# Softmax denominators of a two-layer kernel: partial sums by adding DMAs, one product with ones per pair of heads

## The reference, cut to what matters

```
xn = layernorm(x)                                  # (8, 512, 128)
q = (xn @ Wq + bq).reshape(8, 512, 16, 64); k = xn @ Wk + bk; v = xn @ Wv + bv
w = softmax(einsum('bshd,btd->bhst', q, k) / 8, axis=-1)
out = einsum('bhst,btd->bshd', w, v).reshape(8, 512, 1024) @ Wo + bo
```

## Time and profile before

| | |
|---|---|
| Runs | median 1379.54 us of 3 (1374.84 to 1380.76) |
| Profiled execution | 1377.28 us, its span 1375.2 us, mean granted TensorE clock 0.962 |
| TensorE, matmuls | 91% busy, 7185 instructions |
| VectorE | 74% busy, 2393 instructions |
| ScalarE, GpSimd | 49% and 19% busy |
| DMA | 133.80 MB, mean 97 GB/s |
| Chain that ended last | TensorE 66%, VectorE 21%, issue 5%, ScalarE 3%, DMA 2% |

### The profile page before, as it was taken

One profiled execution on the slowest core, in us unless ns is written; L12 is line 12 of the kernel. 1 busy time (PEld: TensorE's weight loads), 2 busy tenths in 40 slices (PEclk: granted clock), 3 DMA queues, 4 the chain that ended last, 5 costly groups with the idle time before them and its releaser, 6 DMA issues.

```text
span 1375.2 us, 21811 instructions
## 1 busy us (share of the span) xinstructions
PE 1248.2 (91%) x7185; PEld 728.6 (53%) x7185; DVE 1016.0 (74%) x2393; ACT 673.7 (49%) x1252; POOL 262.9 (19%) x314
## 2 busy tenths in 40 slices
PE   4559899998999999999999999999999989999997
PEld 2335445554555455545554555455545558686844
DVE  7777878578857785788587767777677758686875
ACT  3126545534554345434643464345534458676741
POOL 3023222200120012001200120012000206363640
PEclk9559999999999999999999999999999999999999
DMA  2063655222312131224211321132212356465462
GB/s 77 0 169 93 186 170 179 54 58 56 110 46 66 41 116 42 54 49 112 63 49 48 118 64 49 48 90 76 62 44 53 95 162 230 156 227 173 144 203 63
DMA packets 89779, 133.80 MB, mean 97 GB/s; under 512 B 33293, under 2 KB 49229, under 8 KB 85701
## 3 DMA queue, kind: packets, MB, share of 16 engines
q1 hardware_dynamic: 75108, 99.80, 25.5%
q0 software_dynamic: 11344, 31.64, 7.0%
q10 hardware_dynamic: 3216, 0.97, 0.3%
HBM read 59.86 MB, written 38.68 MB: 72 GB/s over the span
## 4 chain that ended last, share of the span: by engine, by line
PE 66%; DVE 21%; issue 5%; ACT 3%; DMA 2%; SPq 2%; POOL 1%; ACTq 0%; DVEq 0%; POOLq 0%
PE bank L1458 14%; PE bank L1430 6%; PE bank L1469 6%; PE bank L1384 5%; PE bank L1431 5%; PE bank L1290 4%; DVE mneg L1022 4%; PE bank L1490 4%; PE bank L1292 4%; PE bank L1291 4%; DVE q_lm L1014 3%; PE bank L1306 2%; PE bank L1296 2%; PE bank L1341 2%; PE bank L1331 1%
## 5 line engine op out<-in xcount | busy, mean ns | idle before, releaser
L844 ACT ACTIVATE wide<-bank 128x512 f32<-128x512 f32 x512 | 296.4, 602 | 470.5 <-PE bank L1431 440.7
L1022 DVE TENSOR_REDUCE mneg<-bank 128x1 f32<-128x512 f32 x512 | 330.0, 685 | 154.5 <-PE bank L1384 147.8
L1458 PE MATMUL bank<-wide,v_w 128*32 128x512 f32 x2048 | 254.1, 615 | 0.8 <-issue 0.8
L1430 PE MATMUL bank<-q_hh,k_hl 128*128 128x512 f32 x512 | 235.7, 460 | 11.0 <-ACT wide L844 9.5
L1431 PE MATMUL bank<-q_lm,k_h 65*128 65x512 f32 x512 | 204.6, 400 | 0.0
L1430 PEld LDWEIGHTS bank<-q_hh,k_hl 128*128 128x128 f32 x512 | 97.1, 190 | 138.3 <-issue 84.0
L636 POOL TENSOR_TENSOR rs<-rs,power 128x4 f32<-128x4 f32 x24 | 24.5, 1021 | 663.3 <-DVE rs L918 663.2
L1469 PE MATMUL bank<-wide,ones 128*32 128x512 f32 x992 | 130.0, 596 | 0.0
L707 POOL DMA_INDIRECT y_rows<-y_m,to_u x92 | 99.1, 1077 | 128.6 <-DVE y_m L1148 106.6
L1458 PEld LDWEIGHTS bank<-wide,v_w 128*32 128x32 f32 x2048 | 54.5, 111 | 126.6 <-issue 121.4
L1384 PE MATMUL bank<-k_b,q_x 128*128 128x512 f32 x256 | 104.1, 407 | 9.6 <-issue 5.1
(11 more groups left out here) (238 smaller groups left out, 1953.3 us busy)
## 6 DMA issues: line engine op xcount, KB each, us to landing
q_hh<-q_x SPq DMA_DIRECT2D x256, 128.0 KB
w_t<-w_rows SPq DMA_DIRECT2D x23, 1024.0 KB
x_rows<-part_h POOLq DMA_DIRECT2D x65, 258.0 KB, 5.0
inv<-inverse_scratch SPq DMA_DIRECT2D x124, 128.0 KB, 3.0
w_rows<-w_t SPq DMA_DIRECT2D x8, 1024.0 KB, 5.1
x_m<-x_rows SPq DMA_DIRECT2D x23, 258.0 KB
stage<-in_L_ffn_W SPq DMA_DIRECT2D x16, 256.0 KB, 4.7
yab<-y_rows POOLq DMA_DIRECT2D x8, 512.0 KB, 7.7
```

What stands on the lines that cost most here:

```text
L844: act.activation(wide[:, st.g % WIDE, :], ps, ACT.Exp, scale=SCALE1).then_inc(wide_full, 1)
L1022: dve.tensor_reduce(mneg[:, pair % 2, col:col + 1], ps[:], X, ALU.max, negate=True).then_inc(free, 1)
L1430: pe.matmul(ps, k_hl[:, n, t], q_hh[:, gh % HEADS, :], start=True, stop=False)
L1458: pe.matmul(ps_out[0][rows, :], v_w[:, n, c, TILE * d:TILE * d + TILE], weights, start=(c == 0), stop=(c == TT - 1))
```

## The change

In the first 54 pairs (`added`) the four quarters' exponentials are added up before they meet the ones. The first quarter of both heads is written into `total`, two buffers of 128x2x512 that lie where `part_h` lies (the expert tiles' buffer, not in use yet). GpSimd adds the other three quarters to it with DMAs that add, 512 KB each, inside SBUF. These wait for each other. `sum_of_added` makes one product with ones of the finished total, as four column tiles (head, half of the queries) of 256 queries; it stands in front of the next pair's first values. `wide` now holds three quarters of a pair in its 6 slots, and ScalarE waits for both the values' product and the addition before it writes a slot again. The sums' copy, store and load are half as large, the addition on VectorE goes, and the rest of the denominators' way comes two steps later (`SUM_LATER`; the second part of `project` too). GpSimd's roots, scatters, fills and subtractions stand at steps (`ROOT_AT`, `SCATTER_AT`, `ZERO_AT`, `SPLIT_STEPS`) among the additions, which are issued 6, 8 and 10 steps behind the pair's first (`ADD_AT`). Four entries of `L0_DVE` move by one or two steps, and some small buffers share memory to make room. The last 10 pairs are computed as before.

```diff
+    ADDED = (NB - 1) * (H // 2) - 2
+    ADD_AT = {6: 1, 8: 2, 10: 3}
+    SUM_LATER = 2
+    WO_AT = [ATT - 10, ATT + 20]
...
-    L0_DVE = [-14, -11, -11, -10, -7, -6, -4, -2, 0, 0, 9, 10, 13, 17, 18, 21, 25, 26, 29, 30, 30, 31, 32,
-              33, 34, 37, 38, 39, 40, 42, 43, 44, 44]
+    L0_DVE = [-14, -13, -11, -10, -7, -6, -4, -2, 0, 0, 9, 10, 13, 17, 18, 21, 25, 26, 29, 30, 30, 32, 32,
+              33, 34, 37, 38, 39, 40, 42, 42, 44, 44]
...
+    ROOT_AT = [30, 42, 51]
+    SCATTER_AT = [[3, 5, 7, 9], [17, 19, 21, 23]]
+    LAST_SCATTER_AT = [[0, 0, 0, 0], [1, 1, 1, 1]]
+    ZERO_AT = [25 + 2 * e for e in range(E)]
...
+            def add(pair, c):
+                g = ATT * (pair // (H // 2)) + PAIR * (pair % (H // 2))
+                pool.wait_ge(wide_full, g + 2 * c + 2)
+                if c == 1:
+                    pool.wait_ge(second_done, g + 2)
+                else:
+                    pool.wait_ge(add_done, adds_before(pair, c - 1) * 16)
+                i = wide_at[g + 2 * c]
+                pool.dma_start(total[:, pair % 2], wide[:, i:i + 2, :], accum_op=ALU.add).then_inc(add_done, 16)
...
+            for st in steps:
+                if st.kind != "o":
+                    continue
+                if st.r < NB - 2 and st.k in ROOT_AT or st.r == NB - 2 and st.k in ROOT_AT[0:2]:
                     root()
+                if add_event(st) is not None:
+                    add(*add_event(st))
+                if st.r == 0 and st.k in SPLIT_STEPS:
+                    split_expert(SPLIT_STEPS.index(st.k))
...
                     act.wait_ge(first_full, st.g + 1)
-                    if st.g >= WIDE:
-                        act.wait_ge(second_done, st.g - WIDE + 1)
+                    past = wide_before.get(st.g)
+                    if past is not None:
+                        act.wait_ge(second_done, past.g + 1)
+                        if past.kind == "o" and added(pair_of(past)):
+                            act.wait_ge(add_done, adds_before(pair_of(past), head_at(past.k)[1]) * 16)
+                    if on_sum(st) and pair_of(st) >= 2:
+                        act.wait_ge(summed, pair_of(st) - 1)
...
+            def sum_of_added(pair):
+                free_bank(("ps", pair))
+                pe.wait_ge(add_done, adds_before(pair, TT - 1) * 16)
+                for b in range(2):
+                    for h in range(2):
+                        rows, cols = slice(DK * b + TILE * h, DK * b + TILE * h + TILE), slice(S // 2 * h, S // 2 * h + S // 2)
+                        last = pe.matmul(ps_out[1][rows, 0:S // 2], ones[:], total[:, pair % 2, b, cols], start=True, stop=True)
+                last.then_inc(summed, 1)
...
                 if half == 0:
+                    if pair and added(pair - 1):
+                        sum_of_added(pair - 1)
+                    free_bank(("pv", pair))
...
+                        if added(pair):
+                            last.then_inc(second_done, 1)
+                if added(pair):
+                    return
```

More of the change, by code:

```diff
@@ L164, in last_step, with pair_of, added, on_sum @@
         return g_of[r, PAIR * (h // 2) + PAIR - 2 + h % 2]
+    def pair_of(st):
+        return st.r * (H // 2) + st.k // PAIR
+    def added(pair):
+        return pair < ADDED
+    def on_sum(st):
+        return st.kind == "o" and added(pair_of(st)) and head_at(st.k)[1] == 0
+    wide_at, wide_before, users = {}, {}, [None] * WIDE
+    for st in steps:
+        if st.kind in ("o", "ye") and not on_sum(st):
+            i = len(wide_at) % WIDE
+            wide_at[st.g], wide_before[st.g] = i, users[i]
+            users[i] = st
+    def adds_before(pair, c):
+        return (TT - 1) * pair + c
     def y_of(st):
@@ L183, in pair_end, with add_event @@
         return past.r * (H // 2) + past.k // PAIR
+    def add_event(st):
+        if st.kind != "o":
+            return None
+        for at_, c in ADD_AT.items():
+            pair, s = divmod(ATT * st.r + st.k - at_, PAIR)
+            if s == 0 and 0 <= pair and added(pair):
+                return pair, c
+        return None
     def direct(pair):
@@ L1199, in row_end @@
                     pair = r * (H // 2) + p
-                    if k == PAIR * p + 16 and not direct(pair):
+                    if k == PAIR * p + 16 + (SUM_LATER if added(pair) else 0) and not direct(pair):
                         dve.wait_ge(sums_loaded, 16 * (pair // 2 + 1))
-                        link(dve.tensor_tensor(sums[:, 0, :], sums[:, 0, :], sums[:, 1, :], ALU.add))
+                        if not added(pair):
+                            link(dve.tensor_tensor(sums[:, 0, :], sums[:, 0, :], sums[:, 1, :], ALU.add))
                         dve.reciprocal(sums[:, 0, :], sums[:, 0, :]).then_inc(inverted, 1)
@@ L1465, in values @@
                                 rows = slice(DK * b + TILE * d, DK * b + TILE * d + TILE)
[L1466 removed]
+                                last = pe.matmul(ps_out[1][rows, :], ones[:], weights_of(c, b), start=(c == 0), stop=(c == TT - 1))
                         else:
                             rows = slice(DK * b + TILE * (c % 2), DK * b + TILE * (c % 2) + TILE)
[L1469 removed]
+                            last = pe.matmul(ps_out[1][rows, :], ones[:], weights_of(c, b), start=(half == 0), stop=(half == 1))
                         last.then_inc(second_done, 1)
```

137 lines of the change are left out of this document (80 added, 57 removed).

## The result

The changed kernel takes 1548.13 us (median of 4 runs, 1541.90 to 1560.33) against 1379.09 us before, measured beside it. The ratio is 1.124, with an interval of 1.117 to 1.132: 12% slower, where 1347 us was forecast. The profiled execution has a span of 1540.2 us at a mean granted TensorE clock of 0.899, where the kernel before had 1375.2 us at 0.962. In the table of experiments the median of e6 mixes two fast executions (1446.31 and 1453.84 us, some 1.05 of the kernel before) and two slow ones (1468.74 and 1471.47 us).

What follows compares the result with a forecast made beforehand. TensorE was taken as the bound, VectorE close behind. Per round, 133.82 us with the additions' floor plus 2.7 for GpSimd's queue against 140.78 gave -29 us; with 1 us from smaller copies, 1347 us, range 1300 to 1415.

Steps and rivals of the forecast that it cites:

- The adds: what may give it back: Three serial GpSimd additions per pair, between values products one pair apart, set a shortest interval of 14.25 us.
- F: Shortest possible interval from one pair's values to the next: 1.95 us plus three additions, 14.25 us.
- hand-overs: Five passes from queue to queue in the additions' loop, estimated at 0.11 us each, 0.54 us together.
- sum product: TensorE's product of ones with the finished total, ahead of the next pair's values: 0.54 us.
- D: One 512 KB addition from issue to landing, taken as 4.1 us from plain transfers in the trace.
- lower end of 3.45: Least time in us for one addition to land, reckoned from the bytes of a plain copy.
- the rival's second price: TensorE's clock falls when it stands still for additions: 47 us more if it happens in five intervals a round.
- It decides from ... D = 4.55: Break-even: from D = 4.55 us (F = 15.6) the change loses, then 10 us per 0.1 us of D.
- The products with ones: TensorE's fewer, narrower sums products gain 1.40 us per pair, 75.6 us over 54 pairs.
- Roots: GpSimd's root() ahead of additions in its queue costs +1.1 us at step 30 and +1.5 at step 42.
- Round 0: Sixteen subtractions of 1.28 us in GpSimd's queue each delay at most one addition, under 10 us in all.
- The adds bound: Rival, chance 0.24: the second read makes D 4.95 us and F 16.8, +40 us, 1418 us.

Runs made afterwards that it cites:

- e6: Changed kernel with the product with ones of an added pair four steps later and each total on its own semaphore; 1461.29 us, ratio 1.064.
- e4: Changed kernel with query copies of only 16 of 512 columns from the fourth pair on (other queries stale); 1501.78 us, ratio 1.091.
- e2: Changed kernel without the 162 additions and the waits for them (denominators of the first quarter alone); 1346.62 us, ratio 0.977.
- e1: Changed kernel with no pair added, every pair keeping its products with ones, all else of the change kept; 1362.56 us, ratio 0.988.
- e10: e2 with the inverse denominators and the second output product two steps later; 1319.70 us, ratio 0.957.
- e12: Kernel before the change with only the three moved entries of VectorE's step list; 1366.14 us, ratio 0.990.
- e13: Changed kernel with two additions a pair, the fourth quarter's weights multiplied by ones in the values block; 1403.32 us, ratio 1.012.
- e8: Changed kernel with the 162 additions computed by GpSimd itself and not by adding DMAs; 1533.34 us, ratio 1.110.
- e5: Changed kernel with seven unread half-width products before TensorE's wait for the additions; 1565.78 us, ratio 1.135.

## Why the prediction was wrong

The failing step is "The adds: what may give it back": the form of the bound was right, "an interval cannot be shorter than F", and each of its four terms was too small, three of them by much. F was put at 14.25 us, which three intervals of a round fall short of; it measured 18.83 us, which six do.

| term of F, us | forecast | chain of I_2 |
|---|---|---|
| half block of values | 0.87 | 0.92 |
| three additions | 12.3 | 15.03 |
| hand-overs | 0.54 | 1.80 |
| sum product | 0.54 | 1.08 |
| F | 14.25 | 18.83 |

- **D.** 4.1 taken, 4.5 measured at the median, with a third addition of 5.1 to 6.4 in five of eight pairs. My reason, "nearest to the one row of the same size and queue (4.3)", chose by likeness of size, and the transfer's kind decided: a copy lands in 2.9, below my lower end of 3.45, and the second read adds 1.6 to it. My 1.5 us for that read was good; I put it into the rival. The query copies, "up to 1.5 us in one of three adds", belonged in the sum: e4 gives 46 us for them.
- **Hand-overs.** "I take 0.11 each", from a semaphore between VectorE and GpSimd's compute. From a release to a DMA's issue on GpSimd it is 0.55. That is 1.26 us in F, and no row of before that I had read showed it.
- **The sum product.** 0.54 us was nearly right at the full clock: 0.64 us in the block at 661.18, after 1.53 us of standing. (Its start-up part of 0.11 us is 0.97 less 0.86 us, not 1.04 less 0.86, as its sentence has it.) After 5.14 us of standing it is 1.08, and the half block of values behind it 1.77 instead of 0.92. I had the fallen clock only as the rival's second price, but a bound interval has it by being bound.
- **"It decides from ... D = 4.55".** With the hand-overs as measured and 0.54 more for the sum it is (15.6 - 0.92 - 1.80 - 1.08) / 3 = 3.93 us. The forecast's own D, 4.1, is above that: with the other terms as measured it gives F = 16.1 us, and a loss.
- **The products with ones.** 1.40 us per pair forecast; in I_0, I_2, I_3 and I_7 e2 shows 1.25, 1.29, 1.22 and 1.30, and less elsewhere. In I_5 even the 1.04 us are the moved list's: e1, with all its products, has 15.8 us there and e2 16.0. Right in size, wrong in "nothing waits for them": in I_1 the inverse denominators' round trip comes out from under the products, and in I_6 VectorE's own work does. That is 136.3 against 129.6 us a round. e10 regains 27 of the 45 us. The reading before it was too kind too: TensorE idles less than 0.3 us in four intervals of the earlier trace rows (I_0, I_1, I_2 and I_4), not in five.
- **The account.** A round was forecast at 133.82 + 2.7 = 136.5 us and took 164.0. By subtraction 6.7 of the 27.5 us are e2's own excess and 20.8 the additions (27.7 by after less e2, where I had 6.9). In the changed kernel itself that round trip is covered again, by the standing for the additions: VectorE waits 4.5 us for the inverse in the whole run. 27.7 x 6.75 = 187 us of e2's 201.5; the other 14 are round 0's, where the additions cost 41.4 us (175.5 against 134.1 in e2), 13.7 more than in a later round.
- **Roots.** "root() at step 30 stands ahead of the first add of I_3": it does, but it ran from 679.00 to 680.03, and the addition was issued at 682.97, late by the slow values block and not by the root. Its +1.1 us was put at the wrong place. In I_3 the second addition is issued 2.06 us behind the landing and not 0.55, with a zero fill between them in the queue; the fill alone doesn't explain it, since one also stands between the second and third addition of I_2, where the hand-over is 0.55 us. Without additions GpSimd's order costs nothing (e12 against e1). **Round 0**, "under 10 us in all": 14 with three additions, some 22 with two.
- **VectorE's list** (three moved entries, not four) got no gain in my sum, "nothing waits". It gives 1% (e12).
- **Rivals.** The adds bound was the right one; its 1418 and 47 more come to 1465, still 83 us short of 1548. It had 0.24, and the range ended at 1415, below it.

## What to carry to other kernels

When a change moves work to a chain of transfers, write the chain as a loop from queue point to queue point with every issue, hand-over and neighbour in it, and compare it with the shortest interval: a loop above it makes every shorter interval pay. e13 shows how sharp this is: the shortest interval takes 12.8 us with two additions and 18.1 with three. When products go that covered a round trip, look for who waited under them. Three moved entries of a list gave what the rest of the change did not.

## What the runs showed of the hardware

- A DMA that adds, 512 KB inside SBUF in packets of 4096 bytes: landing 4.5 us behind the issue at the median (4.4 to 8.6), packets 0.328 us, issue 0.89 us on GpSimd; as a copy 2.9, 0.159 and 0.55 us.
- From a landing to the issue of the next DMA by GpSimd 0.55 us, from a landing to TensorE 0.14 us.
- GpSimd's addition of 128x1024 values takes 2.4 us, and a VectorE instruction with two SBUF inputs beside it, even one of 128x4, lasts to its end (2.64 us for 0.16), while reductions from PSUM keep 684 ns and those from SBUF 520 ns (e8).
- Fillers in front of a wait brought the mean clock from 0.899 to 0.941 and no time (e5, 1565.78 us for 1548.13).
